# Both parts of the weighted values side by side, and inverse square roots as exp(-0.5 ln)

## The reference, cut to what matters

```python
def _layernorm(x, axis=-1, eps=1e-05):
    m = jnp.mean(x, axis=axis, keepdims=True)
    v = jnp.var(x, axis=axis, keepdims=True)
    return (x - m) / jnp.sqrt(v + eps)
# differential attention: 16 heads, Dh = 8, V has 16 columns for each head
A1 = jnp.einsum('bhqd,bhkd->bhqk', Q1, K1) * scaling
A2 = jnp.einsum('bhqd,bhkd->bhqk', Q2, K2) * scaling
attn = softmax(A1) - lam[None, :, None, None] * softmax(A2)      # both causal
O = jnp.einsum('bhqk,bhkd->bhqd', attn, V)
rms = jnp.sqrt(jnp.mean(O * O, axis=-1, keepdims=True) + EPS)     # EPS = 1e-05
O = O / rms * rms_scale * (1.0 - LAMBDA_INIT)
return O @ Wo
# the block
x = x + attn_a(_layernorm(x));  x = x + ffn(_layernorm(x))
x = x + attn_b(_layernorm(x));  x = x + ffn(_layernorm(x))
```

## Time and profile before

| | us |
|---|---|
| median of 3 runs (lowest, highest) | 477.03 (476.18, 477.57) |
| the profiled execution | 479.59 |
| its span, first to last instruction | 477.4 |
| mean granted TensorE clock, as a share of full | 0.957 |

### The profile page before, as it was taken

The page is one execution under the profiler, slowest core; times in us unless marked ns, Lnnn a source line. Parts: engine busy times, 40 slices in busy tenths (PEclk is TensorE's granted clock), DMA queues, the critical chain, the costliest instruction groups (busy, mean ns, idle before and its releaser), DMA issues.

```text
span 477.4 us, 10025 instructions
## 1 busy us (share of the span) xinstructions
PE 414.0 (87%) x3380; PEld 267.7 (56%) x3380; DVE 316.5 (66%) x1139; ACT 261.0 (55%) x608; POOL 222.2 (47%) x332
## 2 busy tenths in 40 slices
PE   1666879978999989998998999896989899999996
PEld 0554635964655555555555555543567666655674
DVE  6575331249888979889897988934144499999311
ACT  2523310211677767676675767778757753354742
POOL 9433310035545647475454747556300577865100
PEclk9988779995899999999999999999899999999999
DMA  8589999907445455544145540000000000000011
GB/s 211 144 252 319 270 268 224 121 2 100 61 56 69 60 67 71 69 62 62 30 56 68 69 69 3 3 3 2 0 2 0 1 0 3 0 1 1 0 45 44
DMA packets 45041, 34.48 MB, mean 72 GB/s; under 512 B 19264, under 2 KB 40896, under 8 KB 43456
## 3 DMA queue, kind: packets, MB, share of 16 engines
q1 hardware_dynamic: 44992, 33.86, 37.4%
HBM read 25.20 MB, written 8.39 MB: 70 GB/s over the span
## 4 chain that ended last, share of the span: by engine, by line
PE 44%; DVE 11%; ACT 9%; issue 8%; POOL 4%; DMA 1%; DVEq 0%; SPq 0%; POOLq 0%; ACTq 0%
PE ps L1005 7%; PE ps L1049 6%; PE ps L1222 5%; PE ps L1026 5%; PE ps L1053 4%; DVE arena L1356 3%; PE ps L1030 2%; PE ps L1008 2%; PE ps L1213 2%; DVE arena L1369 2%; PE ps L1000 2%; PE ps L1126 2%; PE ps L1425 2%; PE ps L1096 2%; ACT arena L806 2%
## 5 line engine op out<-in xcount | busy, mean ns | idle before, releaser
L806 ACT ACTIVATE arena<-ps 128x512 f32<-128x512 f32 x192 | 115.0, 607 | 57.2 <-PE ps L1026 34.7
L758 POOL TENSOR_SCALAR_AFFINE_SELECT arena<-arena 128x256 f32<-128x256 f32 (+1 forms) x192 | 91.2, 485 | 92.8 <-ACT arena L806 91.0
L953 DVE TENSOR_REDUCE arena<-ps 128x2 f32<-128x512 f32 x128 | 85.9, 683 | 8.4 <-PE ps L1008 8.2
L948 DVE CUSTOM_DVE_ANT_0 ps<-ps,future 128x128 f32<-128x128 f32 x256 | 66.4, 320 | 10.8 <-PE ps L1000 9.1
L1297 POOL TENSOR_TENSOR arena<-arena 128x1024 f32<-128x1024 f32 x16 | 34.2, 2137 | 27.8 <-DVE arena L1382 27.3
L1049 PE MATMUL ps<-arena 128*17 128x256 f32 x512 | 40.1, 385 | 0.0
L1008 PE MATMUL ps<-future_bf,ident_bf 128*128 128x256 bf16 x128 | 37.0, 289 | 0.0
L1425 PE MATMUL ps<-arena,upto 128*128 128x384 f32 x96 | 36.0, 487 | 0.3 <-DVE arena L1356 0.3
L948 DVE DVE_READ_ACCUMULATOR2_ANT arena<- 128x1 f32 x256 | 35.6, 139 | 0.0
L388 POOL TENSOR_TENSOR qk_parts_sb<-qk_rest,qk_parts_sb 128x512 bf16<-128x512 f32 x16 | 19.1, 1211 | 30.6 <-DVE qk_parts_sb L492 30.6
L1222 PE MATMUL ps<-w,arena 128*128 128x128 f32 x256 | 30.3, 276 | 1.7 <-ACT arena L1189 1.2
(11 more groups left out here) (148 smaller groups left out, 836.8 us busy)
## 6 DMA issues: line engine op xcount, KB each, us to landing
qk_parts<-qk_parts_sb SPq DMA_DIRECT2D x16, 384.0 KB, 4.2
stack<-qk_parts SPq DMA_DIRECT2D x24, 256.0 KB, 6.8
arena<-qk_parts SPq DMA_DIRECT2D x24, 256.0 KB, 6.8
arena<-in_L_ffn_fc_B_dram SPq DMA_DIRECT2D x4, 1024.0 KB, 7.5
arena<-in_L_ffn_fc_A_dram SPq DMA_DIRECT2D x16, 256.0 KB, 5.0
xs<-in_L_attn_a_X_dram SPq DMA_DIRECT2D x4, 256.0 KB, 4.0
qk_parts<-qk_parts_sb SPq DMA_DIRECT2D x8, 128.0 KB, 4.7
out_dram<-xs SPq DMA_DIRECT2D x4, 256.0 KB, 2.3
```

The source lines that it names most:

```text
L758: nc.gpsimd.affine_select(out=diag, in_=diag, compare_op=ALU.is_ge, fill=0.0, base=0, pattern=[[0, 2 if s < 2 else UMAPS], [1, P]], channe ...
L806: nc.scalar.activation(probs[:, r, s, :], ps[:, bank, :], ACT.Exp, scale=SCALE).then_inc(exp_done, 1)
L948: last = nc.vector.tensor_tensor_reduce(out=block, in0=block, in1=future[:], scale=1.0, scalar=LOWEST, op0=ALU.add, op1=ALU.max, accum_out ...
L953: last = nc.vector.tensor_reduce(out=rowmax[:, gs, 1, at:at + 2], in_=ps[:, bank, :].rearrange("p (m k) -> p m k", m=2), axis=AX, op=ALU.max)
```

## The change

On TensorE both parts of the product with the values stand behind s = 1. Inverse square roots are computed as exp(-0.5 ln(v + eps)), both on ScalarE; `Ln`, `Exp` and what the attention needs else lie in one table, which `load_log_exp` loads. For the rows of `O` that is `inverse_root`, in slot 20 of the sequence, and the factor 1/16 of the mean moves into the squares (0.25 is its root). The steps behind it come one slot earlier, and the tail has 15 slots. For the layer norms `block_log` and `block_rstd` run on ScalarE, and `block_shift` (the product with the mean) stays on VectorE.

```diff
-L_DEN, L_DIFF, L_SQ, L_MS, L_NORM, L_OPT, L_OPROJ, L_STAT = 16, 17, 19, 19, 22, 22, 23, 23
-ROOT_STEPS, ROOT_FIRST = 11, 2
+L_DEN, L_DIFF, L_SQ, L_MS, L_ROOT, L_NORM, L_OPT, L_OPROJ, L_STAT = 16, 17, 19, 19, 20, 21, 21, 22, 22
...
+        def load_log_exp(act):
+            nc.scalar.preload_act_table_set("natural_log_exp_and_others")
...
-                    nc.scalar.activation(std[:, c], moments[:, c, 1], ACT.Sqrt, bias=eps[:, 0:1]).then_inc(std_done, 1)
-                load_table(act, ACT.Exp)
+                    nc.scalar.activation(log_var[:, c], moments[:, c, 1], ACT.Ln, bias=eps[:, 0:1]).then_inc(log_done, 1)
+                    act.wait_ge(log_done, i + 1)
+                    nc.scalar.activation(rstd[:, c], log_var[:, c], ACT.Exp, scale=-0.5).then_inc(rstd_done, 1)
...
+            def inverse_root(it, j):
+                b = seq(it, j, L_ROOT)
+                if (j - L_ROOT) % UPS == 0 and live(b, SEQS):
+                    act.wait_ge(ms_raw, FIRST + b + 1)
+                    nc.scalar.activation(msum, msum, ACT.Ln, bias=eps[:, 0:1]).then_inc(ms_log, 1)
+                    act.wait_ge(ms_log, b + 1)
+                    if past(b):
+                        act.wait_ge(normed, FIRST + b)
+                    nc.scalar.activation(mrms, msum, ACT.Exp, scale=-0.5).then_inc(root, 1)
...
-                    if s < TPS and live(unit(it, j, L_PV), UNITS):
-                        weigh_values(it, j, s)
+                    if s == 1 and live(unit(it, j, L_PV), UNITS):
+                        for t in range(TPS):
+                            weigh_values(it, j, t)
...
-        def block_rstd(dve, S, *blocks):
+        def block_rstd(act, S, *blocks):
             for k in blocks:
                 c = slice(BT * k, BT * k + BT)
-                dve.wait_ge(S["std"], k + 1)
-                nc.vector.reciprocal(rstd[:, c], std[:, c]).then_inc(S["rstd"], 1)
+                act.wait_ge(S["log"], k + 1)
+                nc.scalar.activation(rstd[:, c], log_var[:, c], ACT.Exp, scale=-0.5).then_inc(S["rstd"], 1)
...
                     if slot == TAIL - 3:
-                        block_std(act, F1, 0, 1, 2)
+                        block_log(act, F1, 0, 1, 2)
+                        block_rstd(act, F1, 0, 1, 2)
...
                     if slot == TAIL + 1:
                         feed_gelu_scalar(act, F1, 0)
+                        load_log_exp(act)
                     if slot == TAIL_OUT:
+                        load_table(act, ACT.Gelu_apprx_tanh)
                         feed_rows_scalar(act, F1, 2)
                         feed_gelu_scalar(act, F1, 1)
                         feed_columns_scalar(act, F1, 2)
...
                     if slot == 3:
                         act.wait_ge(F1["mom"], 2 * BLOCKS)
-                        block_std(act, L, 2, 3)
-                        load_table(act, ACT.Exp)
+                        block_log(act, L, 2, 3)
+                        block_rstd(act, L, 2, 3)
...
                     if slot == TAIL - 2:
                         dve.wait_ge(scoredT, BANKS_U * UNITS)
-                        block_rstd(dve, F1, 0, 1, 2)
+                        block_shift(dve, F1, 0, 1, 2)
```

More of the change, by code:

```diff
@@ L31 @@
 DV = 2 * DH
+ROOT_OF_INV_DV = 0.25
 MAPS = 2 * HEADS
@@ L500, in _ @@
                 first_moments(3)
-                for i in range(1, 4):
-                    first_rstd(i)
                 split(0, 0)
@@ L734, in normalise @@
                 if (j - L_NORM) % UPS == 0 and live(b, SEQS):
-                    pool.wait_ge(root, FIRST + ROOT_STEPS * (b + 1))
+                    pool.wait_ge(root, FIRST + b + 1)
                     nc.gpsimd.tensor_tensor(
@@ L898, in mean_squares @@
                     if past(b):
-                        dve.wait_ge(root, FIRST + ROOT_STEPS * b)
+                        dve.wait_ge(root, FIRST + b)
                     nc.vector.tensor_reduce(out=msum, in_=o_n.rearrange("p t h d -> p (t h) d"), axis=AX,
                                             op=ALU.add).then_inc(ms_raw, 1)
-                    dve.wait_ge(ms_raw, FIRST + b + 1)
-                    nc.vector.tensor_scalar(msum, msum, 1.0 / DV, RMS_EPS, op0=ALU.mult,
-                                            op1=ALU.add).then_inc(ms_done, 1)
-            def root_step(it, j, point):
-                for step in range(ROOT_STEPS):
-                    at = 2 + step
-                    lag = L_MS + at // POINTS
-                    b = seq(it, j, lag)
-                    if at % POINTS != point or (j - lag) % UPS or not live(b, SEQS):
-                        continue
-                    dve.wait_ge(root, FIRST + ROOT_STEPS * b + step)
-                    if step == 0:
-                        dve.wait_ge(ms_done, b + 1)
-                        nc.vector.tensor_scalar(root_half, msum, -0.5, None, op0=ALU.mult)
-                        last = nc.vector.tensor_scalar(root_tmp.bitcast(I32), msum.bitcast(I32), 1, None,
-                                                       op0=ALU.logical_shift_right)
-                    elif step == 1:
-                        if past(b):
-                            dve.wait_ge(normed, FIRST + b)
-                        last = nc.vector.tensor_scalar(mrms.bitcast(I32), root_tmp.bitcast(I32), -1.0,
-                                                       float(ROOT_SEED), op0=ALU.mult, op1=ALU.add)
-                    elif (step - ROOT_FIRST) % 3 == 0:
-                        last = nc.vector.tensor_tensor(root_tmp, mrms, mrms, op=ALU.mult)
-                    elif (step - ROOT_FIRST) % 3 == 1:
-                        last = nc.vector.tensor_tensor(root_tmp, root_tmp, root_half, op=ALU.mult)
-                    else:
-                        last = nc.vector.scalar_tensor_tensor(out=mrms, in0=root_tmp, scalar=1.5, in1=mrms,
-                                                              op0=ALU.add, op1=ALU.mult)
-                    last.then_inc(root, 1)
             def emit(it, j):
@@ L966, in emit @@
                     mean_squares(it, j)
-                    for s in range(BANKS_U):
-                        root_step(it, j, s)
                 b = seq(it, j, L_DEN)
@@ L1143, in feed_sems, with block_log, block_shift @@
         def feed_sems(tag):
-            return {k: sem(f"{tag}_{k}") for k in "std rstd ln xn xT xnT up gelu down res st mom stored".split()}
+            return {k: sem(f"{tag}_{k}") for k in "log rstd ln xn xT xnT up gelu down res st mom stored".split()}
         F1, F2 = feed_sems("f1"), feed_sems("f2")
-        def block_std(act, S, *blocks):
+        def block_log(act, S, *blocks):
             for k in blocks:
                 c = slice(BT * k, BT * k + BT)
-                nc.scalar.activation(std[:, c], moments[:, c, 1], ACT.Sqrt, bias=eps[:, 0:1]).then_inc(S["std"], 1)
-        def block_rstd(dve, S, *blocks):
+                nc.scalar.activation(log_var[:, c], moments[:, c, 1], ACT.Ln, bias=eps[:, 0:1]).then_inc(S["log"], 1)
+        def block_rstd(act, S, *blocks):
             for k in blocks:
                 c = slice(BT * k, BT * k + BT)
-                dve.wait_ge(S["std"], k + 1)
-                nc.vector.reciprocal(rstd[:, c], std[:, c]).then_inc(S["rstd"], 1)
+                act.wait_ge(S["log"], k + 1)
+                nc.scalar.activation(rstd[:, c], log_var[:, c], ACT.Exp, scale=-0.5).then_inc(S["rstd"], 1)
+        def block_shift(dve, S, *blocks):
+            for k in blocks:
+                c = slice(BT * k, BT * k + BT)
                 dve.wait_ge(S["rstd"], k + 1)
@@ L1249, in hybrid_kernel @@
         oT_l, at = carve(at, (2, TPS * P))
-        names = ("std rstd ln xn xT xnT qkv neg exp phi v kv pre prod nd inv oraw o oT oTs out res st mom").split()
+        names = ("log rstd ln xn xT xnT qkv neg exp phi v kv pre prod nd inv oraw o oT oTs out res st mom").split()
         L = {k: sem(f"l_{k}") for k in names}
```

61 lines of the change are left out of this document (27 added, 34 removed).

## The result

| | before | after |
|---|---|---|
| median (lowest, highest) | 476.77 (476.18, 477.57), 4 runs | 471.76 (468.84, 473.29), 4 runs |
| the profiled execution | 479.59 | 473.29 |
| its span | 477.4 | 471.1 |
| granted TensorE clock, mean | 0.957 | 0.952 |

The ratio of the times is 0.988, 95% interval 0.984 to 0.991. A second set of runs, beside others of the kernel before, gave 471.85 for 477.95 (0.987, 0.984 to 0.989): 5 to 6 us faster, where 9.1 were forecast. (The first set has one run of the kernel before more than the table ahead of the prediction.) The 471.8 lies inside the range, 3.9 above the predicted 467.9. The profiled executions differ by 6.3.

A forecast was written before the change was run, and what follows sets the result against it. The prediction took TensorE to bound the attention. Its terms, A to H, summed to -9.1 us against the profiled 479.59, giving 470.5, or 467.9 for the median, with a range of 462.5 to 474.5.

The forecast's parts named there:

- term B: Attention: putting both parts of the product with the values side by side saves 0.23 us in 57 slots, -13.1 us.
- Rival 1: Attention: the fixed time belongs to the small products, so joining saves nothing; +4.0 us, 481.0; chance 0.06.
- Rival 2: Attention: the exponentials become the bound, each slot loses some 0.1 us, 473.6; chance 0.12.
- a rival that the prediction had dismissed: Attention: VectorE could take back the gain; its share put at most 0.85, against 0.87 before; no chance given.
- Term C: Attention, once-a-sequence step, six times: normalisation comes sooner, but the output projection waits for ScalarE's copy; net +0.5 us.
- D: Attention's tail slot 4: the inverse root's logarithm and exponential on ScalarE, which sets the pace there; +0.5 us.
- Term A: First stage: a table load and its one-column activation go, an exponential comes, most of the lead passes on; -1.0 us.
- Term F: F1's last block: its rows come behind the inverse root and a load of gelu's table; +2.8 us.
- Term E: Start of F1's rows: VectorE's shifts stand behind the residual and statistics of sequence 6; +1.5 us.
- G: Three places where ScalarE is ahead of a stage: an exponential there replaces VectorE's reciprocal; +0.4 us.
- H: Linear stage: four reciprocals leave a nearly full VectorE; -0.7 us.

The follow-up runs named there:

- the kernel with the cut apart: Kernel before, first part of the product with the values cut by queries into two halves, the second behind the second bank's scores: 491.56 us (1.028).
- the one with the cut together: Kernel before, first part of the product with the values cut by queries into two halves, both in the old place: 478.12 us (0.9995).
- F1's last rows early: Changed kernel, with ScalarE writing the normed rows of F1's block 2 ahead of the last sequence's squares and the gelu table load: 466.62 us (0.977).
- the one edit by itself: Kernel before, with the logarithm and exponential of layer norm in the first stage alone: 476.59 us (0.998).
- the logarithms alone: Changed kernel, with the two parts of the product with the values apart again, as before: 481.43 us (1.007).
- both edits: Changed kernel, F1's block 2 rows and VectorE's shifts early, plus rows of blocks 0 and 1 ahead of ScalarE's copy of a product: 464.27 us (0.972).

## Why the prediction was right and wrong

**What bounds the kernel, and term B: right.** The slot went from 2.88 to 2.65, to the hundredth, and the junction measured by itself costs 0.235 where 0.23 was read from the starts of the matmuls. Both ends that were kept for it (0.09 and 0.42) are excluded.

**Rivals.** Rival 1 would have had the kernel with the cut apart as fast as the one with the cut together, and it is 13.4 us slower. The rule of the Trainium skill named there ("TensorE: Matmul & The Clock Gate", "The mechanism") isn't what decides: eight more weight loads of the same row groups cost nothing in a series. Rival 2, the exponentials as a bound, didn't come in the regular slots. The one slot in eight that takes 2.76 instead of 2.65 is bound by VectorE, a rival that the prediction had dismissed by a share of at most 0.85 over the sequence: such a mean doesn't tell that one long instruction (the reciprocal sums, 0.55) puts the maxima 0.1 too late for TensorE.

**Term C: right in its parts.** The slot of L1108 went from 4.68 to 4.23 (4.14 forecast), that of the projection from 3.87 to 4.05 (4.03 forecast). What the prediction didn't see is that B isn't to be had in the first of these slots without the earlier step: the join without it gives 7.3 us, not 12. B, C and D together were forecast as -12.1 and measured -12.04. That they agree to 0.1 is luck. The changed kernel's sequences take 26.15 where 25.94 was forecast, which over six is 1.3 short; and what made up for it was in no term: the first eight slots took 18.80 instead of 19.45 (19.30 in the profile with F1's last rows early, whose attention is the same), and one sequence of before had taken 28.30, 0.6 more than its like.

**Term A: not settled.** The prediction expected most of the 1.2 us to pass through a chain of projections, stores and loads. The stretch shows -0.1 in place of -1.0, but between two profiles of the changed kernel alone it differs by 2.0; the one edit by itself gives -0.8, give or take 1. So -1.0 may have been right, and the runs don't exclude 0.

**Term F: right in its size, short of its consequence.** The 2.8 came as 2.85, and the wait of about 4 as 4.35. The step that failed is what stands behind the late rows: the sum has no term for this block's products, and so takes them at their old price. After a wait of 4.35 us the 32 products took 5.20 instead of 3.57, +1.63. The profile before had the hint in TensorE's output projection. It takes 1.16 in the loop, and at the attention's end, behind a wait, at a granted clock of 0.58:

```profile
334.01 1.83 PE L1126 MATMUL ps<-wo,arena 128*128 128x128 f32 x8
```

**Term E: right number, by luck, and half of the cause.** +1.55 for +1.5. The rows themselves start 6.2 us after the last exponential, not 5.5: L1097 took 2.0 to the next instruction at the lower clock, which the prediction had as its end of 2.2, and 0.6 was made up before the up-projection. The chain that the prediction wrote out (residual, statistics, shift) ends at 323.85 and so did look like the cause, and with the logarithms alone it is: the rows wait 0.55 for the shifts there. With the parts joined, taking the shifts out of it didn't move the rows, since ScalarE's own queue held them as long: two causes of the same length, and it took both edits to see a gain. The second comes with the join, which alone, without a logarithm, adds 1.44 to this stretch when the output projection runs at the lower clock (L1127 2.08, stretch 10.34); at the full clock, with F1's last rows early, it is 8.33 (L1127 1.16). The prediction had counted the joined products only as a gain.

**G and H** were forecast as -0.3 and are -0.2. From the last early transposes of the linear stage (L1450 at 372.64, its successor at 366.70) to the up-projection of F2 (441.13 and 434.76) are 68.49 and 68.06 us, so H gave 0.4 of its 0.7. What lies before and behind it has grown by 0.2, half of G.

The sum missed by 2.8 us in the profiled execution: 1.6 is the clock behind F, and 0.9 stands in the first stage, less than that stage varies by from one profile to the next.

## What to carry to other kernels

On an engine that is the bound, look at the starts of its instructions for a fixed time wherever the weights change in width or place, and put series of the same kind together; here that was worth 0.235 us for each series less, and cutting them finer cost nothing as long as they stood together. Before a table load or a chain of another engine goes ahead of something that TensorE waits for, look for work of that queue that can pass it: 5.2 us of the change's gain hung on the order of two calls. A mean share of busy time doesn't show the one slot in which an engine off the critical path is late. And when a step is taken out of a chain and nothing moves, look at the queue of the engine that does the next step, before giving up the step.

## What the runs showed of the hardware

The small products write to four groups of partitions and run side by side: two maps take 0.54 us, four take 0.56, and two half series of all four 0.57 together.

TensorE's clock fell behind F1's late rows in each profile that has them. After idle times of 3.60 to 4.41 us, 32 products took 5.2 us, and after 1.51 or none they took 3.6; one of them takes 275 ns before and 274 to 423 ns in the changed kernel. A delay of 2.8 us upstream thus cost 4.5. At the output projection it doesn't always fall: behind waits of the same length, 0.67 and 0.68 for ScalarE's copy, the eight products took 2.08 at a granted 0.50 in one profile and 1.16 at 1.00 in another.

A reload of ScalarE's table costs its 1.28 us and no more: the load at 336.43 ends at 337.71, and the rows behind it and its one column start at 337.83. The Trainium skill ("ScalarE: Activation LUTs", "What ACT_TABLE_LOAD costs") adds a drain of about 1.38 us; the trace shows none here.
